# Projections of the first attention as three f16 products, x split by GpSimd

## The reference, cut to what matters

```python
def _L0_cond_ref(x, mask, Wq, Wo):          # x: 8 x 256 x 512, NH = 8, dk = 32
    xt = jnp.transpose(x, (0, 2, 1))
    q = xt @ Wq.T
    qh = q.reshape(B, T, NH, dk).transpose(0, 2, 1, 3)
    scores = scale * jnp.einsum('bhqd,bhkd->bhqk', qh, qh)
    logits = (scores * cmask + (1.0 - cmask) * NEG) * rmask
    attn = jax.nn.softmax(logits, axis=-1)
    ctx = jnp.einsum('bhqk,bhkd->bhqd', attn, qh)
    ...
    out = ctx @ Wo.T
x = x + _L0_ffn_ref(_L0_cond_ref(x, ...), ...)
```

## Time and profile before

| | us |
|---|---|
| median of 3 runs | 2156.62 (2155.53 to 2160.58) |
| the profiled execution | 2158.13 |
| its span, first to last instruction | 2156.0 |
| PE busy | 1704.8 (79%) |
| PEld busy (weight loads, beside PE) | 1011.0 (47%) |
| DVE busy | 1079.7 (50%) |
| ACT busy | 619.3 (29%) |
| POOL busy | 274.1 (13%) |

### The profile page before, as it was taken

One profiled execution on the slowest core, in us unless ns is written; L12 is line 12 of the kernel. 1 busy time (PEld: TensorE's weight loads), 2 busy tenths in 40 slices (PEclk: granted clock), 3 DMA queues, 4 the chain that ended last, 5 costly groups with the idle time before them and its releaser, 6 DMA issues. The chain is left out here.

```text
span 2156.0 us, 33026 instructions
## 1 busy us (share of the span) xinstructions
PE 1704.8 (79%) x10731; PEld 1011.0 (47%) x10731; DVE 1079.7 (50%) x2009; ACT 619.3 (29%) x1152; POOL 274.1 (13%) x343
## 2 busy tenths in 40 slices
PE   5788888883059999356787787795599999999998
PEld 1232323321036666132344444354477777777776
DVE  5455555543433333134455555553466665665665
ACT  0343333441332222221433434341321111111111
POOL 3111111101822222201111111000000000000000
PEclk7899999996579999756798998996699999999999
DMA  4122221102944444611111111114500000000000
GB/s 147 45 55 55 54 54 54 40 11 82 356 141 83 82 82 82 174 50 30 32 39 40 39 39 39 22 29 95 133 1 10 10 0 10 10 10 0 10 10 10
DMA packets 113345, 122.00 MB, mean 57 GB/s; under 512 B 40389, under 2 KB 79193, under 8 KB 113209
## 3 DMA queue, kind: packets, MB, share of 16 engines
q1 hardware_dynamic: 96872, 86.63, 14.2%
q0 software_dynamic: 15632, 34.30, 7.6%
q10 hardware_dynamic: 768, 0.13, 0.0%
HBM read 61.17 MB, written 29.96 MB: 42 GB/s over the span
## 5 line engine op out<-in xcount | busy, mean ns | idle before, releaser
L1770 ACT ACTIVATE d_SG<-d_bank 128x256 f32<-128x256 f32 x264 | 101.4, 384 | 380.6 <-PE d_bank L1707 301.6
L301 DVE TENSOR_REDUCE a_NM<-a_bn 128x1 f32<-128x512 f32 x256 | 163.3, 685 | 83.9 <-PE a_bn L215 80.6
L1805 DVE SCALAR_TENSOR_TENSOR d_HF<-d_bank,d_SG 128x256 f32<-128x256 f32 x264 | 112.2, 425 | 170.6 <-ACT d_SG L1770 152.3
L283 ACT ACTIVATE a_EX<-a_bt 128x512 f32<-128x512 f32 x256 | 143.9, 596 | 149.5 <-PE a_bt L234 149.1
L252 PE MATMUL a_bc<-a_EX,a_V 128*64 128x512 f32 x512 | 143.1, 638 | 0.0
L215 PE MATMUL a_bn<-a_B,a_A 97*128 97x512 f16 x256 | 99.4, 421 | 46.6 <-DVE a_NM L301 28.8
L1812 DVE TENSOR_TENSOR d_H_l<-d_HF,d_H_h 128x256 f16<-128x256 f32 x264 | 112.4, 426 | 9.0
L234 PE MATMUL a_bt<-a_A,a_B 98*128 98x512 f16 x256 | 91.7, 388 | 19.3 <-ACT a_EX L283 17.4
L301 DVE TENSOR_REDUCE c_NM<-c_bn 128x2 f32<-128x512 f32 x128 | 81.0, 681 | 44.9 <-PE c_bn L215 41.2
L864 PE MATMUL b_TX<-identh,R 128*128 128x128 f16 x312 | 24.2, 221 | 91.7 <-DVE b_wdl L1020 90.3
L215 PEld LDWEIGHTS a_bn<-a_B,a_A 97*128 97x128 f16 x256 | 22.6, 98 | 157.6 <-DVE a_NM L301 113.6
(11 more groups left out here) (346 smaller groups left out, 4013.6 us busy)
## 6 DMA issues: line engine op xcount, KB each, us to landing
R<-slot_rows SPq DMA_DIRECT2D x39, 264.0 KB, 2.7
b_stage<-in_L_ffn_w_gate SPq DMA_DIRECT2D x8, 704.0 KB, 7.4
b_stage<-in_L_ffn_w_up SPq DMA_DIRECT2D x8, 704.0 KB, 7.1
a_xb<-in_x SPq DMA_DIRECT2D x8, 512.0 KB, 3.6
a_A<-a_H SPq DMA_DIRECT2D x64, 64.0 KB, 2.9
a_B<-a_H POOLq DMA_DIRECT2D x64, 64.0 KB, 2.6
a_CT<-a_CS SPq DMA_DIRECT2D x32, 128.0 KB
b_stage<-in_L_ffn_w_down SPq DMA_DIRECT2D x8, 512.0 KB, 5.4
```

Source lines behind the costliest of these rows:

```text
L283: nc.scalar.activation(self.EX[s % 4][:, :], self.bt[s % 2][:, :], ACT.Exp).then_inc(self.exp_done, 1)
L301: self.nc.vector.tensor_reduce(self.NM[:, s * cols:(s + 1) * cols], self.bn[s % 2][:, :].rearrange("p (k n) -> p k n", k=cols), AX, ALU.ma ...
L1770: nc.scalar.activation(SG[k % 3][:, :], GU[(f + 3) % 4][:, 0:CH], ACT.Silu, scale=1.0 / WS).then_inc(silu, 1)
L1805: V.scalar_tensor_tensor(out=HF[:, :], in0=b[:, CH:2 * CH], scalar=1.0 / WS, in1=SG[k % 3][:, :], op0=ALU.mult, op1=ALU.mult).then_inc(mul ...
```

## The change

x and the transposed weight Wq are split into f16 high and low parts. VectorE splits the weight once, scaled by WS = 64. GpSimd splits x of each batch with a cast and a subtraction into two-buffered tiles xh and xl. In the opening it splits batches 0 and 1 ahead of its fills, and later the split of batch n + 1 follows the mask rows of batch n. q and values become three f16 products each, high by high, low by high and high by low, in place of one f32 product. The scale is taken out again in VectorE's instructions that read the results. SP's load of x waits additionally for the split of two batches before.

```diff
+        xh = [sb(f"xh{i}", [P, 2, T0], F16) for i in range(2)]
+        xl = [sb(f"xl{i}", [P, 2, T0], F16) for i in range(2)]
+        wqh, wql = sb("wqh", [P, 2, S0], F16), sb("wql", [P, 2, S0], F16)
...
                 else:
+                    sp.wait_ge(x_lo, n.idx - 1)
                     sp.wait_ge(a.v_ready, n.idx - 1)
...
             @block.gpsimd
             def _(pool):
+                def split_x(n):
+
+                    pool.wait_ge(x_in[n.par], 32 * (n.half + 1))
+                    if not n.first and not (isinstance(n.idx, int) and n.idx == 1):
+                        pool.wait_ge(a.v_ready, n.idx - 1)
+                    pool.sem_inc(split_begun, 1)
+                    nc.gpsimd.tensor_copy(xh[n.par][:, :, :], xb[n.par][:, :, :]).then_inc(x_hi, 1)
+                    pool.wait_ge(x_hi, n.idx + 1)
+                    nc.gpsimd.tensor_tensor(xl[n.par][:, :, :], xb[n.par][:, :, :], xh[n.par][:, :, :],
+                                            ALU.subtract).then_inc(x_lo, 1)
+                    pool.wait_ge(x_lo, n.idx + 1)
+
+                split_x(Batch(0, 0))
+                split_x(Batch(0, 1))
                 for k, (buf, value) in enumerate(((a.B[0][96:98, :, :], c.shift_scale), (a.B[1][96:98, :, :], c.shift_scale),
                                                   (a.V[0][:, :, :, :], 1.0), (a.V[1][:, :, :, :], 1.0))):
                     nc.gpsimd.memset(buf, value).then_inc(ones_set, 1)
...
                 rows(Batch(0, 0))
                 rows(Batch(0, 1))
-                with pool.Fori(0, NB // 2 - 1) as i:
+                split_x(Batch(0, 2))
+                with pool.Fori(0, NB // 2 - 2) as i:
                     for q in range(2):
                         rows(Batch(i, q + 2))
+                        split_x(Batch(i, q + 3))
+                rows(Batch(NB // 2 - 2, 2))
+                split_x(Batch(NB // 2 - 2, 3))
+                rows(Batch(NB // 2 - 2, 3))
...
                 pe.wait_ge(w_out, 2)
+                pe.wait_ge(wq_lo, 1)
...
-                    pe.wait_ge(x_in[n.par], 32 * (n.half + 1))
+                    pe.wait_ge(x_lo, n.idx + 1)
                     bank = a.pe_take(pe, uses)
                     for k in range(2):
-                        mm = nc.tensor.matmul(bank[:, :], wT[:, 0, k, o * P:(o + 1) * P], xb[n.par][:, k, :],
-                                              start=(k == 0), stop=(k == 1))
+                        for m, (w, xs) in enumerate(((wqh, xh), (wql, xh), (wqh, xl))):
+                            mm = nc.tensor.matmul(bank[:, :], w[:, k, o * P:(o + 1) * P], xs[n.par][:, k, :],
+                                                  start=(k == 0 and m == 0), stop=(k == 1 and m == 2))
...
                             for k in range(2):
-                                mm = nc.tensor.matmul(bank[:, t * S0:(t + 1) * S0],
-                                                      xb[n.par][:, k, (2 * u + t) * P:(2 * u + t + 1) * P],
-                                                      wT[:, 0, k, :], start=(k == 0), stop=(k == 1))
+                                for m, (xs, w) in enumerate(((xh, wqh), (xh, wql), (xl, wqh))):
+                                    mm = nc.tensor.matmul(bank[:, t * S0:(t + 1) * S0], xs[n.par][:, k, toks], w[:, k, :],
+                                                          start=(k == 0 and m == 0), stop=(k == 1 and m == 2))
...
+                dve.wait_ge(w_out, 2)
+                nc.vector.tensor_scalar(wqh[:, :, :], wT[:, 0, :, :], WS, None, ALU.mult).then_inc(wq_hi, 1)
+                dve.wait_ge(wq_hi, 1)
+                nc.vector.scalar_tensor_tensor(out=wql[:, :, :], in0=wT[:, 0, :, :], scalar=WS, in1=wqh[:, :, :],
+                                               op0=ALU.mult, op1=ALU.subtract).then_inc(wq_lo, 1)
                 dve.sem_inc(turned_free, 1)
...
-                    chain.did(nc.vector.scalar_tensor_tensor(out=QM[:, :], in0=bank[:, :], scalar=QSCALE,
+                    chain.did(nc.vector.scalar_tensor_tensor(out=QM[:, :], in0=bank[:, :], scalar=QSCALE / WS,
                                                              in1=cb[n.par][:, :], op0=ALU.mult, op1=ALU.mult))
...
-                        nc.vector.tensor_copy(a.V[n.par][:, 2 * u:2 * u + 2, :, 0:32],
-                                              bank[:, :].rearrange("p (t h d) -> p t h d", t=2, h=c.heads)).then_inc(a.proj_out, 1)
+                        nc.vector.tensor_scalar(a.V[n.par][:, 2 * u:2 * u + 2, :, 0:32],
+                                                bank[:, :].rearrange("p (t h d) -> p t h d", t=2, h=c.heads),
+                                                1.0 / WS, None, ALU.mult).then_inc(a.proj_out, 1)
```

More of the change, by code:

```diff
@@ L389, in layer0_attention @@
         rows_done = sem("rows_done")
+        x_hi, x_lo, wq_hi, wq_lo = sem("x_hi"), sem("x_lo"), sem("wq_hi"), sem("wq_lo")
+        split_begun = sem("split_begun")
         XTh = sb("XTh", [P, KF, S0], F16)
@@ L497, in values @@
                         for t in range(2):
+                            toks = slice((2 * u + t) * P, (2 * u + t + 1) * P)
                             for k in range(2):
-                                mm = nc.tensor.matmul(bank[:, t * S0:(t + 1) * S0],
-                                                      xb[n.par][:, k, (2 * u + t) * P:(2 * u + t + 1) * P],
-                                                      wT[:, 0, k, :], start=(k == 0), stop=(k == 1))
+                                for m, (xs, w) in enumerate(((xh, wqh), (xh, wql), (xl, wqh))):
+                                    mm = nc.tensor.matmul(bank[:, t * S0:(t + 1) * S0], xs[n.par][:, k, toks], w[:, k, :],
+                                                          start=(k == 0 and m == 0), stop=(k == 1 and m == 2))
                         mm.then_inc(a.proj_made, 1)
```

## The result

The changed kernel takes 2164.3 us (median of 16 runs) against 2157.1 for the kernel before: a ratio of 1.0033, 95% interval 1.0021 to 1.0045. The prediction said 2164.1 and slower. The profiled run took 2162.34 us, 4.2 more than the one of before.

What follows compares the result with a forecast made beforehand. TensorE and its hand-offs were taken to pace settled batches, a chain to first scores the opening; +14.2 - 0.6 - 5.2 - 0.9 = +7.5 us gave 2164.1 us, 8-in-10 range 2155 to 2175.

Steps and rivals of the forecast that it cites:

- Part 1: Opening: GpSimd's fills, moved behind two splits, hold VectorE's first take of q up by 14.2 us.
- Part 2: q as six f16 products: 5.2 us saved over batches 2 to 7, and 0.6 in batch 1.
- Part 3: Values: 1.1 us gross saved eight times, but the transposed scores wait for the row-of-shifts DMA, so only 0.9 us counts.
- rival (a): Values' saving is kept because the row of shifts lands within 2.0 us of its issue: 2157.3 us, chance 0.15.
- Part 4: Settled batches: load waits, later splits, longer unrolled end and additional semaphores cost nothing.
- Rival (b): More idle TensorE behind boundaries brings one more half-clock stretch in each of six batches, 10 us: 2174, chance 0.15.
- Rival (d): Products limited by weight loads rather than columns would save nothing: 2170 us, chance 0.03.
- Rival (c): Five half-clock stretches gone give 8.5 us, a subtraction costing only a copy 2.1 more: 2153.5, chance 0.07.

Runs made afterwards that it cites:

- fills_first: The changed kernel with GpSimd's four fills put ahead of the splits of batches 0 and 1 again: 2154.6 us, ratio to before 0.9986.
- fills_late: The kernel before, with GpSimd waiting for x of batches 0 and 1 ahead of its fills, no split: 2168.5 us, ratio 1.0046.
- values_f32: The changed kernel with values back as f32 products of the unsplit x: 2162.9 us, ratio to before 1.0022.
- pv_late: first_f32 with the last product of weights and values of each pass moved behind the transposition of the maxima: 2156.9 us, ratio to before 0.9995.
- split_twice: The changed kernel with each split of batches 2 to 7 made twice on GpSimd, once into spare tiles: 2162.9 us, ratio to before 1.0023.
- values_one: The changed kernel with only the first (high by high) of the three products of values: 2174.9 us, ratio to before 1.0091.
- first_f32: The changed kernel with fills first and batch 0 from f32 x: 2150.7 us, ratio to before 0.9966; run again unchanged, 2152.1 us, 0.9972.
- q_only: first_f32 with values as f32 products of the unsplit x in all batches: 2148.0 us, ratio to before 0.9961.

## Why the prediction was right

**Part 1, the fills behind the splits**, is the term that decides, and it was right in mechanism and size: +14.2 predicted, 13.98 measured at VectorE. The fills began at 17.59 and ended at 28.4 (predicted 17.85 and 28.7). The subtraction that the trace of before didn't show took 2.12 us; I had taken 2.1, twice the copy, between bounds of 1.04 and 4.2. The factor of two was a guess between these bounds, which allowed a delay of 12.1 to 18.4, and that it came so close is luck. The estimate from the Trainium skill (GPSIMD Engine Reference, "Elementwise — side-by-side cycle accounting"), 2.25 us for two f32 inputs, is 6% longer than this subtraction, one of whose inputs is f16. At the scores the delay was only 13.06, as the last DMA of the assembly landed 1.8 us behind its issue (42.32 to 44.10), where it had been 2.6 (28.44 to 31.04). fills_first and fills_late show that it is the order: the one takes 8.8 of the 14.0 us away, the other makes 10.0 of them without a split.

**Part 2, q**, was right. Six products start 0.215 apart and a full-clock batch is 0.7 to 1.3 us shorter than before, predicted 0.9 to 1.0. With 1.7 us taken off for each stretch, the five passes between the second and the seventh L224 average 56.05 us before and 55.15 after. In batch 1 the scores came 20.70 us behind L224 instead of 21.41: 0.7 against my 0.6. One detail differed: VectorE's second q step came 0.94 sooner behind L224, not 0.45. The clock had risen by then (q1's products start 0.215 apart from 69.74 on), so that step waited for VectorE's first, and not for TensorE.

**Part 3, values**: gross 1.1 us a batch saved, next to nothing kept, as predicted: the idle behind the products is 0.6 to 1.3 us at six boundaries, and values_f32 is no slower. Summed over the seven boundaries, the transposed scores begin 27.1 us behind L224 before and 26.2 after, so 0.9 us was kept, the very figure of my sum. Where it was kept I hadn't foreseen: 0.9 came at the one boundary where the DMA of before had landed latest (171.70) and 0.7 at the last, while three others lost 0.2 to 0.4. So rival (a) is out. pv_late adds a second cover that I hadn't seen: with the wait for the DMA gone, SyncE's queue and the reciprocal held the time.

**Part 4**: nothing, shown by split_twice. Settled splits ran at 137.49 where the load, shifted with the batch, put them, and q came more than 20 us later.

**The sum** was +7.5 and the medians differ by 7.2. That agreement is closer than my terms deserve. In the profile 5.8 us came back behind the opening, where I had 6.7 (0.6, 5.2 and 0.9), and the opening itself was 1.1 short of its term; the 5.8 also contain half-clock stretches, which the two profiles have in different places and lengths; by the estimate above for them it would be 6.6. The opening's missing 1.1 and the interval of the measurement, 4.5 to 9.7 us, still leave the agreement of the sums to luck. Rival (b), more stretches, didn't come true in this pair of profiles: five behind batch 1's opening in each, and only the one in that opening longer, 13.6 us against 6.8. values_one shows that longer idle and more of the lower level come together. Rival (d) is out with the spacing of 0.215 and 0.11; by its own terms, with q and values saving nothing, its time would have been 2170.8. Rival (c) has its number too: the two profiles of first_f32 differ by six stretches with no edit at all.

## What to carry to other kernels

Work that an engine does while it must wait for a load anyway is free only as long as it stands ahead of the first instruction that waits for the load; a new preparation step belongs behind it, and the first batch, where nothing covers that step, may be better off without it. Before a product is made cheaper, follow what ends last at its place: a DMA in flight took nearly the whole of the values' saving, with a queue of issues behind it, while the same trick paid at q, where an engine waited for that product. And where removed work turns into idle time ahead of heavy work, look at the granted clock: with 2 us of idle and more it cost more here than the work had.

## What the runs showed that I had not expected

A small cast of VectorE beside GpSimd's work can be stretched severalfold. In q_only, by the timeline of the opening:

```profile
14.95 2.13 POOL L459 TENSOR_TENSOR a_xl<-a_xb,a_xh 128x1024 f16<-128x1024 f32 x1
15.42 1.94 DVE L648 CAST a_H<-a_QM 128x512 f16<-128x512 f32 x1
```

The cast of 128x512 takes 0.43 us elsewhere (L640 of the changed kernel at 29.26) and here 1.94, ending 0.28 us behind the subtraction's end; the subtraction has its usual 2.13. The two engines seem to share something that GpSimd held. The Trainium skill (SBUF — State Buffer, "SBUF: two separate sides") tells of a port pair that is held as a lock and not divided, and these rows agree. VectorE's next step, 0.69, is as long as elsewhere. The changed kernel has a smaller case: VectorE's product of 32 columns at 10.95 takes 0.99 us beside GpSimd's cast (10.86 to 11.90), where it took 0.19 before, and the one ahead of it, with GpSimd still idle, takes 0.17 where it had taken 1.54 beside the fill. In first_f32 the cast of q takes 1.68, which is part of why its scores come later. It is 1.2 to 1.5 us once; in settled batches the split lies where VectorE has no such cast.

The other is the size of the clock's share: nine stretches against three between two executions of one kernel, and up to 25 us at stake in values_one. Beside these the whole change, 7 us, is small.
